# A recurrent stage and a score stage put into one block, with the states transposed by PE where they lie

## The reference

```python
for p in range(1, MAX_SKIP + 1):                 # MAX_SKIP = 4
    nw = Tv // p
    wins = h[:, :nw * p, :].reshape(Bv * nw, p, Hd)
    last = _lstm_last(Wih[p - 1], Whh[p - 1], bih[p - 1], bhh[p - 1], wins)
    h = h.at[:, jnp.arange(nw) * p + (p - 1), :].set(last.reshape(Bv, nw, Hd))
...
x = x + h
h = relu(layernorm(x))
Xq = (h @ W_lin.T).reshape(bt, n, heads, dh)
Xv = (h @ W_val.T).reshape(bt, n, heads, dh)
e = einsum('behd,hd->beh', leaky_relu(Xq[:, src] + Xq[:, dst], 0.2), a)
```

## Time and profile before

| what | value |
|---|---|
| time, median of 3 runs | 1326.67 us (1326.37 to 1327.11) |
| the profiled execution | 1325.95 us |
| its span, first to last instruction | 1324.1 us |
| mean granted TensorE clock | 0.963 of full |
| busy over the span | PE 1207.0, DVE 1046.4, ACT 943.9, POOL 380.6 us |
| recurrent stage's last hidden state | ends at 1014.59 us of the span |
| first projections of the score stage | 1030.70 us |

### The profile page before, as it was taken

One profiled execution on the slowest core, in us unless ns is written; L12 is line 12 of the kernel. 1 busy time (PEld: TensorE's weight loads), 2 busy tenths in 40 slices (PEclk: granted clock), 3 DMA queues, 4 the chain that ended last, 5 costly groups with the idle time before them and its releaser, 6 DMA issues. The chain is left out here.

```text
span 1324.1 us, 23335 instructions
## 1 busy us (share of the span) xinstructions
PE 1207.0 (91%) x6740; PEld 973.4 (74%) x6740; DVE 1046.4 (79%) x2069; ACT 943.9 (71%) x1745; POOL 380.6 (29%) x770
## 2 busy tenths in 40 slices
PE   3999978979879998999999999999996999967898
PEld 2999975643368886788879888977984777745777
DVE  4787767986768876988798879878875799958885
ACT  1666648867668886877787778767765899835675
POOL 3577650000067430000000000000001566627775
PEclk8999998999969999999999999999998899988999
DMA  8000000000031110000000000003003000000112
GB/s 296 1 0 0 0 0 0 0 0 0 4 132 71 63 49 1 0 1 0 1 0 1 0 1 1 1 0 127 1 0 127 2 0 1 1 0 24 73 64 96
DMA packets 14466, 37.88 MB, mean 29 GB/s; under 512 B 1856, under 2 KB 3904, under 8 KB 13120
## 3 DMA queue, kind: packets, MB, share of 16 engines
q1 hardware_dynamic: 13008, 36.31, 7.2%
q10 hardware_dynamic: 1392, 0.74, 0.2%
HBM read 20.27 MB, written 16.78 MB: 28 GB/s over the span
## 5 line engine op out<-in xcount | busy, mean ns | idle before, releaser
L955 ACT ACTIVATE gates<-bank,lstm_bias 128x512 f32<-128x512 f32 (+1 forms) x504 | 301.6, 636 | 101.5 <-PE bank L944 88.3
L139 ACT ACTIVATE l_h<-X,nmr,rstd 128x128 f32 (+1 forms) x512 | 210.3, 485 | 54.2 <-POOLq L133 32.8
L108 POOL TENSOR_TENSOR l2r_sum<-l2r_st 128x8 f32<-128x8 f32 x16 | 3.3, 208 | 532.2 <-DVE l2r_st L89 531.9
L929 PE MATMUL bank<-lstm_node_hi,Wih_hi 128*128 128x512 f32 (+1 forms) x408 | 149.4, 366 | 0.0
L930 PE MATMUL bank<-lstm_node_hi,Wih_lo 128*128 128x512 f32 (+1 forms) x408 | 149.0, 365 | 0.0
L931 PE MATMUL bank<-lstm_node_lo,Wih_hi 128*128 128x512 f32 (+1 forms) x408 | 148.8, 365 | 0.0
L940 PE MATMUL bank<-lstm_hid_hi,Whh_hi 128*128 128x512 f32 (+1 forms) x288 | 104.1, 362 | 4.4 <-DVE lstm_hid_hi L1011 4.3
L944 PE MATMUL bank<-lstm_hid_lo,Whh_hi 128*128 128x512 f32 (+1 forms) x288 | 106.9, 371 | 0.0
L941 PE MATMUL bank<-lstm_hid_hi,Whh_lo 128*128 128x512 f32 (+1 forms) x288 | 103.2, 358 | 0.0
L960 ACT ACTIVATE gates<-lstm_cell 128x512 f32<-128x512 f32 (+1 forms) x144 | 83.7, 581 | 21.6 <-DVE lstm_cell L998 21.1
L931 PEld LDWEIGHTS bank<-lstm_node_lo,Wih_hi 128*128 128x128 f32 x408 | 77.2, 189 | 11.7
(11 more groups left out here) (253 smaller groups left out, 3315.4 us busy)
## 6 DMA issues: line engine op xcount, KB each, us to landing
X<-in_x SPq DMA_DIRECT2D x8, 1024.0 KB, 14.8
x_spill<-X SPq DMA_DIRECT2D x32, 256.0 KB, 2.0
X<-x_spill SPq DMA_DIRECT2D x2, 4096.0 KB, 12.5
out<-X SPq DMA_DIRECT2D x32, 256.0 KB, 2.0
w_raw<-in_WihT SPq DMA_DIRECT2D x1, 1024.0 KB, 5.6
w_raw<-in_WhhT SPq DMA_DIRECT2D x1, 1024.0 KB, 7.8
W<-in_L_W ACTq DMA_DIRECT2D x1, 192.0 KB, 5.1
rows<-in_rows ACTq DMA_DIRECT2D x1, 128.0 KB, 4.4
```

The source lines that it names most:

```text
L139: last = act.activation(h[:, j, :], k.X[:, bass.ds(b0, TB), :][:, j, :], ACT.Relu, bias=k.nmr[:, bass.ds(b0, TB)][:, j:j + 1], scale=k.rst ...
L929: pe.matmul(out, hi, x_high, start=True, stop=False)
L955: act.activation(gate_of(it, g), k.bank[4 * s + g][:, 0:it.N], ACT.Tanh if g == GATE_G else ACT.Sigmoid, bias=k.lstm_bias[:, it.p - 1, g:g ...
```

## The change

Both stages become one block (`stage_lstm_and_scores`), without the barrier and the clearing of semaphores between them; `stage_scores` becomes a class `Scores` whose parts are called in each queue. Its buffers are placed over those of the recurrent stage: h, hT, Xq, Qs over its x halves and the like, the score buffers over its weights.

- PE: before the matmuls of the last item it transposes the states for turn 0 into two gate banks of slot 0; those for turn 1 follow the item, and the turns of the score stage follow that.
- DVE: before the cell of the last item it adds the states of turn 0 to X and takes the statistics. The update for turn 1 follows the last hidden state.
- ACT: normalises slot 0 of turn 0 before the tanh of the last item, slot 1 behind it.
- PE transposes the states straight from HT; ACT's copy L583 is gone in this stage, and the buffer l2r_o with it.
- All 16 turns are written out, in place of the loops; the steps of semaphores that the loops needed go. SP asks for the second half of X when both slots are done.

```diff
+    def turn_over(self, pe, i, s):
+        if i:
+            pe.wait_ge(self.R["updated"][s], i)
+        for j in range(TB):
+            b = (i * self.S + s) * TB + j
+            last = pe.transpose(self.psR[s][:, j * P:(j + 1) * P], self.states[:, b // GROUP, :, b % GROUP], self.k.ident[:, :])
+        last.then_inc(self.R["R"][s], 1)
+
+    def update(self, dve, i, tail_in):
+        X, R = self.k.X, self.R
+        if i == self.tail_at:
+            dve.wait_ge(tail_in, 16)
+        for s in range(self.S):
+            xt = X[:, self.rows(i, s), :]
+            dve.wait_ge(R["R"][s], i + 1)
+            dve.tensor_tensor(xt, as_tile(self.psR[s]), xt, ALU.add).then_inc(R["updated"][s], 1)
+        for s in range(self.S):
+            dve.wait_ge(R["updated"][s], i + 1)
+            self.ln.stats(dve, X[:, self.rows(i, s), :], s, i)
+
+    def normalise(self, act, i, s):
+        self.ln.wait(act, s, i)
+        normalise_tile(act, self.k, self.h[s], (i * self.S + s) * TB).then_inc(self.R["h"][s], 1)
...
 # SP
+            for s in range(S):
+                sp.wait_ge(computed[s], ends[s].n + 1)
+            sp.dma_start(k.X[:, head:, :], k.x_spill[:, head:, :]).then_inc(x_tail, 16)
...
 # PE
             for it in items:
                 s = it.slot
+                if it is items[-1]:
+                    pe.wait_ge(act_out[0], gate_count(ends[0], GATE_O))
+                    for r in range(sc.S):
+                        sc.turn_over(pe, 0, r)
...
+            pe.wait_ge(act_out[1], gate_count(ends[1], GATE_O))
+            sc.on_tensor(pe)
...
 # ACT
+            sc.normalise(act, 0, 0)
             tanh_of_cell(before)
+            sc.normalise(act, 0, 1)
+            sc.on_scalar(act)
...
 # DVE
+                if it is items[-1]:
+                    dve.wait_ge(x_head, 16)
+                    sc.update(dve, 0, x_tail)
                 new_cell(it)
...
             new_hidden(before)
+            sc.on_vector(dve, x_tail)
...
 # ACT, the turn before and after
-                if place:
-                    for s in range(S):
-                        act.wait_ge(res.R_ready[s], i + AHEAD + 1)
-                        res.fetch(act, s, fetched(place, (AHEAD + 1) * S + s))
...
 # PE, the turn after
+        for i in range(1, AHEAD):
+            for s in range(S):
+                self.turn_over(pe, i, s)
+        for i in range(n_it):
+            for s in range(S):
+                pe.wait_ge(R["h"][s], i + 1)
+                for j in range(TB):
+                    last = pe.transpose(psT[s][:, j * P:(j + 1) * P], h[s][:, j, :], k.ident[:, :])
+                last.then_inc(R["Tp"][s], 1)
+                if i + AHEAD < n_it:
+                    self.turn_over(pe, i + AHEAD, s)
```

More of the change, by code:

```diff
@@ L57, in each, with as_tile @@
     return [make(i) for i in range(n)]
+def as_tile(ps):
+    return ps[:, :].rearrange("p (b n) -> p b n", b=TB)
 class LayerNormTail:
@@ L849, in gate_count, with stage_lstm_and_scores @@
     return it.gates_before + it.gates.index(g) + 1
-def stage_lstm(k, ctx, HT):
+def stage_lstm_and_scores(k, ctx, HT, e, w_at):
     nc = k.nc
@@ L869, in stage_lstm @@
         for n in ("done", "act", "cell", "tanh", "vec", "computed", "hi", "lo", "xh", "xl"))
-    x_head = k.sem("lstm_x_head")
+    x_head, x_tail = k.sem("lstm_x_head"), k.sem("lstm_x_tail")
+    sc = Scores(k, ctx, HT, e, k.nc.sbuf_base - 8 * 4 * TW, w_at)
     groups = k.B // GROUP
@@ L897, in x_halves @@
         return [columns(it, part[it.tile % 2][it.slot]) for part in (x_hi, x_lo)]
+    ends = [[it for it in items if it.slot == s][-1] for s in range(S)]
     with nc.Block() as block:
@@ L907, in _ @@
             sp.dma_start(k.X[:, 0:head, :], k.x_spill[:, 0:head, :]).then_inc(x_head, 16)
+            for s in range(S):
+                sp.wait_ge(computed[s], ends[s].n + 1)
+            sp.dma_start(k.X[:, head:, :], k.x_spill[:, head:, :]).then_inc(x_tail, 16)
             sp.wait_ge(x_head, 16)
+            sp.wait_ge(x_tail, 16)
+        @block.gpsimd
+        def _(pool):
+            sc.on_pool(pool)
         @block.tensor
@@ L1035, in _ @@
             new_hidden(before)
+            sc.on_vector(dve, x_tail)
+    return sc.scores, sc.Xv
 def stage_edges(k, ctx, e):
@@ L1437, in stage_attend @@
     PER_CHUNK = tiles // sm.NQ
-    as_tile = lambda ps: ps[:, :].rearrange("p (b n) -> p b n", b=TB)
     tile_of = lambda buf, t: buf[:, t * TB:(t + 1) * TB, :]
@@ L1654, in build @@
             with ExitStack() as c2:
+                w_at = nc.sbuf_base
                 sbr = lambda n, s: c2.enter_context(nc.sbuf_tensor(n, s, F32R))
@@ L1660, in build @@
                 with ExitStack() as c:
-                    stage_lstm(k, c, HT)
-            k.recycle_semaphores()
+                    scores, Xv = stage_lstm_and_scores(k, c, HT, e, w_at)
             with ExitStack() as c3:
-                sb3 = lambda n, s: c3.enter_context(nc.sbuf_tensor(n, s, F32))
-                e.q_sums = sb3("q_sums", [P, B * k.HEADS])
-                scores, Xv = sb3("scores", [P, EC, B * k.HEADS]), HT[:, :].rearrange("p (b n) -> p b n", n=P)
-                with ExitStack() as c:
-                    stage_scores(k, c, HT, Xv, scores, e)
+                c3.enter_context(nc.sbuf_tensor("kept_scores", [P, (1 + EC) * B * k.HEADS], F32))
                 with ExitStack() as c:
```

241 lines of the change are left out of this document (101 added, 140 removed).

## The result

| what | before | after |
|---|---|---|
| time, median | 1326.89 us (4 runs, 1326.37 to 1328.29) | 1319.38 us (4 runs, 1317.89 to 1319.56) |
| ratio | | 0.9941, 95% interval 0.9927 to 0.9955 |
| span of the profiled execution | 1324.1 us | 1317.6 us |
| last hidden state starts | 1013.90 | 1020.82 |
| first QV starts | 1030.70 | 1024.79 |

What follows compares the result with a forecast made beforehand. PE was taken to be full in the score stage's turns, with DVE full too once the copy goes. Seam -7.8, copies -2.0 and strided transposes +12.7 gave +2.9 us, from 1326.67 to 1329.6; range 1315 to 1333.

Steps and rivals of the forecast that it cites:

- The bound: Score stage, full turn: without ACT's copy PE needs 8.75 us and DVE 8.77, so PE has no room.
- ACT's copies, -2.0: Score stage, turns 1 to 12: removing ACT's copies of the states saves 0.17 us a turn, -2.0 us.
- The strided transposes, +12.7: Score stage, turns 3 to 15: loads of strided states take 0.230 us, 0.122 more for each of 104 transposes, +12.7 us.
- The seam, -7.8: Between recurrent and score stage: putting the first residual before the last item starts the first QV 7.8 us earlier.
- Turn 0, 0 forecast: First turn of the score stage: keeps its 9.80 us, no change.
- Rival 1: Score stage: PE's strided weight load is hidden, its term vanishes, -9.8 us, time 1316.9; chance 0.34.

Runs made afterwards that it cites:

- the tanh first: Changed kernel with ACT's tanh of the last item ahead of both normalisations of turn 0: 1316.08 us, ratio 0.9926 to the kernel before.
- two blocks: Changed kernel with its turns in a block of their own behind a barrier, first residual after it: 1323.69 us, ratio 0.9976 to the kernel before.
- three other orders: Changed kernel with last tanh before both normalisations (1316.08 us), turn 0's residual one item earlier (1315.03), or that plus turn 1's before the last item (1312.75).

## Why the prediction was wrong

**The bound.** Right. PE has no room in a turn: eight more transposes cost 0.906 us, all on the path.

**ACT's copies, -2.0.** Right, and for the reason given. The copy's wait returns with the copy. 0.17 us less eight times the 0.0035 us that a transpose grew is 0.14 a turn, which is what the run measured.

**The strided transposes, +12.7. This step failed.** It said that 128 groups at the pace of PE's fastest stream take 0.230 us, that ACT's 0.98 us for the same addresses confirms it, and that everything beyond 0.108 us is exposed. Measured is 0.112 us a transpose (1068.65 to 1069.10) against 0.108 before, so 104 x 0.004 = +0.4 us. The number itself was not absurd: a plain matmul's load at these distances took 0.204 to 0.224 us. But it is not this instruction's number. The row that I took for PE's port was the moving side of a plain matmul, and ACT's was another engine; what roughly carries over is the ratio of strided to contiguous (2.0 for PE's moving side, 1.9 for its plain load, 1.7 for a transpose's load and for ACT, 1.5 for DVE), not the time. Applied to the transpose's own load (at most 0.068 us contiguous), a ratio of 1.9 gives an estimate of 0.13, 0.02 over the matmul's time: a term of some +2 us instead of +12.7, and a gain on the whole. I had a hint in hand: the load records of the earlier trace rows are 140 ns for a transpose, while the group of G's loads, plain fp32 matmuls whose weights also lie side by side, has a mean of 190 ns in the same trace (groups of PE's weight loads before, 1030 to 1160):

```profile
L1269 PEld LDWEIGHTS bank<-l_Xq,PT 128*128 128x128 f32 x114 | 19.5, 190 | 23.1 <-issue 11.0 <-ACT l_Xq L1232 9.2 <-ACT Y L1234 2.9
```

50 ns between two loads of 128 numbers suggest that the two kinds of load don't take the same time, and so that a price for one need not be one for the other.

The Trainium skill, "SBUF — State Buffer", paragraph on cachelines, says that a line must be hit twice for full bandwidth. With the exposed loads the runs agree for PE's plain loads, 0.112 us at distance 2 and 0.221 at 4, but not for a transpose's, which pays at 2 already (0.126 against 0.068). Its example of four fp32 apart as still free is not borne out: at 4 PE's plain load, ACT (1.10 against 0.61) and DVE (1.06 against 0.69) all pay in full. The prediction leaned on the rule for the fact that there is a price; the mistake was to add where it says nothing, in the size. The Trainium skill, "TensorE: Matmul & The Clock Gate", section on LDWEIGHTS, gives columns divided by 1.2 as the load's ns, 107 for 128 columns. The plain load agrees at granted clock 1.00 (0.106; at 0.50 it took 0.216), the transpose's (0.068) is shorter. An estimate by the page's figure doubled, 0.213 us, would have kept most of the forecast's term, +11 us.

**The seam, -7.8.** The mechanism was right, the size 0.84 us off. The chain from the end of the statistics (1011.17 + 1.63 = 1012.80) to the first normalisation (1018.54) took 5.74 us, not the 4.40 of before. POOL's additions stood beside DVE's cell, whose operands all lie in SBUF, and the run with POOL alone and beside DVE shows that this slows them (1.31 to 4.06 us for eight) and that an operand in PSUM or statistics, which stood beside them before, do not. The statistics themselves ended 0.75 us later than forecast, but slot 0's state, from which the stretch is counted, came 1.05 later. From the first transpose to the first QV it took 4.55 us, not 4.75. So the 0.84 are 1.34 of POOL less 0.30 and 0.20.

**Turn 0, 0 forecast, +0.26 measured.** The first QV ran longer at the lower clock: the granted clock is 0.50 for 2.7 us from its start (to 1027.5), before for 2.2 us (1030.70 to 1032.9), and it takes 5.01 us against 4.78. POOL was just in time, as forecast: its last coefficients end at 1028.63, ACT normalises from 1028.71 on and had not stood. With the tanh first and the QV at granted clock 1.00, the stretch is 8.78 us.

**What no step held.** +1.05 us lie ahead of all changed code. The traces of the kernel before and of the seven that were timed against it put slot 0's state between 1001.45 (before) and 1003.09 (two blocks), the six others from 1001.63 to 1002.75, with the same work ahead of it; that it varies so much among them speaks against the change as its cause. The difference is made early: the same matmuls start 0.2 us later after the change at 32 us of the span, 0.7 at 206 and 1.2 at 376. PE's clock is a likely part of it, not a shown one: after the change it is granted 0.50 up to 37.6 us, before only up to 36.2, and it rises earliest in the kernel before and latest in the one of two blocks (38.1). +0.84 us lie in the attend stage, also unchanged. There PE is granted 0.50 from 1170 to 1175 and its first eight transposes take 1.97 us, where they took 1.09 before. In all eight traces the stage's length goes with its mean granted clock: 147.5 us at 0.94; 148.0, 148.1 and 148.3 at 0.93; 148.9 twice at 0.92; 149.5 and 150.3 at 0.91. That is a strong sign that the clock is the reason, but no run set the clock by itself. So a difference of about a microsecond between two of these kernels' times need not come from the code.

**The chances.** Rival 1 was given 0.34 against 0.52 for the forecast. Its sum, -9.8, holds up to the terms above: -6.96 + 0.26 - 1.69 = -8.39 from changed code. Its reason, a load that fits under the matmul, is what the runs showed. The range held the result only because it was drawn to hold rival 1 too.

## What to carry to other kernels

When an engine is to read strided numbers, carry over the ratio, as a rough one, and not the time, and start from that instruction's own contiguous time: a transpose whose load nearly doubles can still be hidden under its matmul (0.111 us at distance 16 against 0.108), a short plain matmul can't. A copy that exists only to make data contiguous for a transpose by PE is a candidate for removal (0.14 us a turn here, 1.7 us in all in the trace, too little to see in the kernel's time), above all where PE is full and the copy holds up something else. When two stages are overlapped, look at what now runs beside POOL's small operations, and put the last tanh, on which everything later waits, ahead of work that is itself still waiting: three other orders made the seam and turn 0 2.3 to 4.4 us shorter. And cut the traces into stretches before a microsecond is put down to the code: here unchanged stages moved by as much.

## What the runs showed of the hardware

- POOL's additions of 128x8 run at a third of their speed beside DVE operations whose two inputs lie in SBUF (4.06 us for eight against 1.31), and untouched (1.30) beside operations with one input in PSUM or beside statistics. The Trainium skill, "SBUF — State Buffer", section "SBUF: two separate sides", describes a port pair that DVE with two SBUF inputs and a GpSimd operation that reads SBUF can only hold one at a time; the three figures agree, and the seam's records of 1.09 and 0.65 us are what it does to a kernel.
- ACT and DVE pay for distance from four numbers on: 1.10 and 1.06 us against 0.61 and 0.69; at 2 they pay 0.04 and 0.00 us.
- At granted clock 0.50 a plain load by PE of numbers 16 apart takes 0.220 us (48 in 10.58), two apart 0.217; at 0.89 to 1.00 it takes 0.204, two apart 0.112. Here the strided load hardly depended on the clock while the contiguous one doubled (0.106 to 0.216), so a measurement at the lower clock hides what distance costs.
- The exposed load of a transpose of 16 partitions is shorter than that of a plain fp32 matmul of 128 partitions, 0.068 us against 0.106, and nearly doubles already at distance 2 (0.126), where the plain one does not (0.112).
- The attend stage, the same code in eight kernels, took 147.5 us at a mean granted clock of 0.94 and 149.5 to 150.3 at 0.91.
